# A two-layer graph network on one core: the edge attributes turned by VectorE in 32 x 32 squares, with a slot of a tile holding 128 consecutive edges

## The chip, the cores and the metric

One core of a Trainium2 chip. The metric is the device time of one execution in microseconds; the span is the part of it between the first and the last instruction that the profile shows. Engines are named TensorE (PE; PEld is its weight load), VectorE (DVE), ScalarE (ACT), GpSimd (POOL) and SyncE (SP).

## The reference

12,500 nodes with 64 features, 200,000 edges sorted by target, 32 attributes per edge. All in float32.

```python
# layer 0
x_t = leaky_relu(x @ W1n + b1n) @ W2n + b2n                 # nodes
e_t = leaky_relu(edge_attr @ W1e + b1e) @ W2e + b2e         # edges: 32 -> 64 -> 64
agg = segment_sum(x_t[src] * e_t * dp_scale, dst)
x   = layernorm(x + (layernorm(x + agg * res_w) * gamma + beta))
# layer 1: 8 relations, weights from 4 bases
xw  = x @ (w_comp @ weight)                                 # one table of rows per relation
agg = segment_sum(xw[edge_type, src] * edge_weight, dst)
out = layernorm(x + relu(agg + h_bias))
```

## The kernel before

A **tile** is 512 edges, J = 4 **slots** of 128, one edge to a partition. 390 whole tiles are worked off in 195 **pairs** (V = 2 tiles), and a tail of 320 edges is the 196th. Ten tiles are a **body**, five pairs a **half**; each loop iteration is two halves. In the kernel before, partition p of a tile holds the four consecutive edges 4p to 4p+3, one in each slot.

**Before the edges.** The node network fills `node_table` in HBM. Meanwhile the lists `dst`, `src`, `edge_type` and `edge_weight` are loaded, 512 to a row, cast by GpSimd, and turned by TensorE (`turn`, L1272 to L1279), so that an edge's number comes to lie on its partition; VectorE makes the target numbers relative to the tile's first (`relative`), ScalarE copies the sources and weights out of PSUM, VectorE makes the row numbers of layer 1 (`row_of`). The sources of the first ten tiles come by a DMA of their own straight into `src_ix`, so that gathers can begin as soon as `node_table` is written.

**Layer 0, one step per pair p.** The five engines run the same order of steps, written out by hand, and meet by semaphores only:

- GpSimd (`gather`, L571): four indirect DMAs per tile bring 128 rows of 256 bytes each into one of ten slots of `rows`. A tile may be fetched when the message of the tile ten before is made (`msg_ready`).
- SyncE (L425): loads the attributes of a half (640 KB) into one of two halves of `attr`, when those of the half before it in the same place are turned.
- TensorE (`step0`, L1376 and after): scatters pair p, tile by tile (L1347: messages times one-hot, summed over the edges, into PSUM); second matmuls of the edge network for pair p+2 (L1332 for the bias, L1339); first matmuls for pair p+3 (L1323, `attrT` against `W1e_d`, into `ps_z`); then turns the attributes of pair p+4 (L1315, two transposes of 128 x 128 into `ps_T`).
- ScalarE (`step`): `low` = 0.1 z + 0.1 b of the first matmuls (L639) for pair p+2, then the copy of the turned attributes of pair p+3 from `ps_T` to `attrT` (L630), by which columns are also put in order.
- VectorE (`step0`, L1147 and after): `hid` = max(z + b, low) for pair p+2 (L1029); message of the odd tile of pair p (L1054: gathered rows times `ps_o`); adds the even tile's sums to `acc` (L983); one-hot of pair p+1 (L972); message of the even tile of pair p+1; adds the odd tile's sums.

`attrT`, `ps_z` and `low` exist once, so the chain first matmuls, `low`, `hid`, second matmuls, first matmuls goes round once per pair. In places fixed by a table of limits (`final`), a chunk of 5 blocks of nodes that can get no further edges is finished between steps: turned, normed (VectorE, 14 steps), and its rows for layer 1 are made in three parts (TensorE `rel_products` against ScalarE `rel_copies`) and stored.

**Layer 1** has no edge network: gathers from `rel_table`, messages, scatter, add, and the last normalisation.

The lines of the step that the change touches:

```python
def edge_copy(p):                                            # ScalarE
    act.wait_ge(transposed, p + 1 if is_fixed(p) else count(p))
    nc.scalar.copy(attrT[...], ps_T[...]).then_inc(attr_copied, 1)

def attr_transpose(p, u, turns):                             # TensorE
    for t in range(width(p)):
        last = nc.tensor.transpose(ps_T[...], attr[..., t * P : (t + 1) * P], ident[:])
    last.then_inc(transposed, 1)
```

Of the kernel before, what the change touches and what calls it, by code (L numbers as in the profile page):

```python
# [5 lines left out]
def bass_gnn_resnorm_d2_kernel(  # L6
# [46 lines left out]
    P = 128  # L53
# [15 lines left out]
    assert TAIL_P * J == E - FULL * ST and 0 < TAIL_P < P  # L69
    BODY = 10  # L70
# [23 lines left out]
    src_begin = src[0 : BODY * ST].rearrange("(s p j) -> p s j", p=P, j=J)  # L94
    weight_flat = edge_weight.rearrange("e o -> (e o)")
    attr_groups = edge_attr[0 : FULL * ST, :].rearrange("(g s p r) k -> g p s (r k)", s=HALF, p=P, r=V * J)
# [3 lines left out]
    with ctx:  # L100
# [54 lines left out]
        x_pair = rows[:, 0, :, :].rearrange("p (k b) f -> p k (b f)", k=2)  # L155
        attrT = sb("attrT", [P, V * P])
# [122 lines left out]
        src_first = sem("src_first")  # L279
        gathered = [[sem(f"gathered{l}_{u}") for u in range(BODY)] for l in range(2)]  # L280
        transposed = sem("transposed")
        attr_copied = sem("attr_copied")
# [118 lines left out]
        def _(sp):  # L401
# [22 lines left out]
            def load_attr(h, g):  # L424
                sp.dma_start(attr[:, h, :, :], attr_groups[g]).then_inc(attr_loaded[h], 16)  # L425
# [31 lines left out]
            def layer0_loads():  # L457
                sp.reg_mov(done, 0)
                with sp.Fori(0, LOOPS - 1) as i:
                    for h in range(2):  # L460
                        sp.wait_ge(transposed, i * TURN + (h + 1) * HALF)
                        load_attr(h, i * 2 + (2 + h))
                        next_chunk(sp, done, limit, i * 2 + h, store_rel)
                sp.wait_ge(transposed, (BODIES - 2) * HALF)
                load_attr(0, BODIES - 1)
                next_chunk(sp, done, limit, BODIES - 3, store_rel)
                sp.wait_ge(transposed, (BODIES - 1) * HALF)
# [13 lines left out]
            sp.dma_start(src_ix[:, :, :], src_begin).then_inc(src_first, 16)  # L481
# [24 lines left out]
        def _(pool):  # L506
# [37 lines left out]
            for q in range(PAIRS):  # L544
# [6 lines left out]
                stage(q)  # L551
                if ZERO_FIRST <= q < ZERO_FIRST + ZERO_PARTS:
# [4 lines left out]
            def gather(l, t):  # L557
# [5 lines left out]
                if l == 0 and t == 0:  # L563
                    pool.wait_ge(src_first, 16)
                if l == 0 and t == BODY:
                    pool.wait_ge(list_taken, 5)
# [19 lines left out]
        def _(act):  # L586
# [28 lines left out]
            node_lower(PAIRS - 1, 0)  # L615
            act.wait_ge(s_edge_const, 16 * len(EDGE_CONSTS))
# [9 lines left out]
            def edge_copy(p):  # L626
                w = width(p) * P
                act.wait_ge(transposed, p + 1 if is_fixed(p) else count(p))
                if width(p) == V:
                    nc.scalar.copy(  # L630
                        attrT[:, :].rearrange("k (t q c) -> k c t q", t=V, c=V),
                        ps_T[:, 0:w].rearrange("k (c t q) -> k c t q", t=V, c=V),
# [902 lines left out]
```

## Time and profile before

| | |
|---|---|
| median of 3 runs | 5004.18 us (4999.41 to 5016.95) |
| profiled execution | 5002.53 us |
| its span | 5000.7 us |
| instructions | 33,996 |
| busy | PE 2157.5, PEld 1454.3, DVE 1585.2, ACT 380.7, POOL 2994.8 us |
| DMA | 175,940 packets, 169.74 MB |
| chain that ended last | another core or an unknown queue 23%, issue 22%, PE 11%, DVE 9% |

The busy time of an engine is the time in which one of its instructions ran; register, branch and semaphore instructions aren't counted. A matmul's end is modelled. "PEclk" is the clock that TensorE was granted, as a share of 2.4 GHz. In a row of the timeline stand the start, the time until the last of the merged instructions ended, engine, line, operation, tiles, shapes and count, and in brackets how long the engine was idle before and what released it; "remote" and "issue" are releasers that the profile can't name.

### The profile page before, as it was taken

What the parts mean: (1) busy time and instruction counts of PE and PEld (TensorE: products, weight loads), DVE (VectorE), ACT (ScalarE), POOL (GpSimd) and SP (SyncE); (2) the same over time, 40 slices, a digit from 0 to 9 for tenths busy, and PEclk for the clock granted to TensorE, in tenths of its full rate; (3) what the DMA queues carried; (4) which work ended last, traced back from release to release, by engine and by line L of the source; (5) the groups of instructions that cost most, each with busy time, mean ns of one, the idle gap of its engine ahead of it and who ended that gap; (6) DMA issues with size and microseconds to landing.
All of it is one profiled execution on the core that took longest, in us unless ns stands there. A gap on an engine that the chain in (4) does not pass through costs nothing.

```text
span 5000.7 us, 33996 instructions
## 1 busy us (share of the span) xinstructions
PE 2157.5 (43%) x7388; PEld 1454.3 (29%) x7389; DVE 1585.2 (32%) x3586; ACT 380.7 (8%) x879; POOL 2994.8 (60%) x3219
## 2 busy tenths in 40 slices
PE   6444454555555555565555233332333332232323
PEld 5333333333333433343332111121222221121222
DVE  4222232323333333343332122232322233233234
ACT  2100010101111111111111000000000000000000
POOL 5566665556555655555543676667666666666654
PEclk7777776777777777776775555555555555555556
DMA  4111111111111111121111111111111111111111
GB/s 101 29 32 32 32 33 42 31 43 42 42 41 38 45 42 46 32 52 41 51 37 39 23 25 22 24 23 25 23 25 25 25 24 25 24 24 26 25 25 21
DMA packets 175940, 169.74 MB, mean 34 GB/s; under 512 B 84098, under 2 KB 111606, under 8 KB 175630
## 3 DMA queue, kind: packets, MB, share of 16 engines
q0 software_dynamic: 100096, 102.60, 11.6%
q1 hardware_dynamic: 75246, 64.45, 4.2%
q14 instruction: 299, 2.45, 0.2%
q8 instruction: 11, 0.18, 0.0%
q10 hardware_dynamic: 288, 0.07, 0.0%
HBM read 134.80 MB, written 32.10 MB: 33 GB/s over the span
## 4 chain that ended last, share of the span: by engine, by line
another core or an unknown queue 23%; issue 22%; PE 11%; DVE 9%; DVEq 8%; ACT 1%; POOL 1%; ACTq 0%; DMA 0%; SPq 0%
PE ps_agg L1347 4%; DVE acc L983 3%; DVEq L965 2%; DVE work L1054 2%; DVE work L972 2%; PE ps_fin L1431 1%; PE ps_o L1339 1%; DVEq L983 1%; PE ps_z L1323 1%; DVEq L996 1%; DVEq L987 1%; PE ps_agg L1431 1%; POOL rows L571 1%; PE ps_T L1420 1%
## 5 line engine op out<-in xcount | busy, mean ns | idle before, releaser
L571 POOL DMA_INDIRECT rows<-node_table,acc x1524 | 1441.6, 946 | 1029.5 <-DVE work L1054 587.8
L571 POOL DMA_INDIRECT rows<-rel_table,row_ix x1564 | 1479.1, 946 | 886.1 <-issue 467.3
L1347 PE MATMUL ps_agg<-work 128*128 128x256 f32 x2348 | 906.9, 536 | 1658.1 <-DVE work L1054 1239.9
L1347 PEld LDWEIGHTS ps_agg<-work 128*128 128x128 f32 x2348 | 573.5, 265 | 1942.2 <-DVE work L1054 1324.1
L972 DVE TENSOR_TENSOR work<-ps_x,rel 128x1024 f32<-128x1024 f32 x392 | 479.0, 1222 | 535.9 <-issue 425.0
L983 DVE TENSOR_TENSOR acc<-acc,ps_agg 64x128 f32 x1174 | 333.7, 284 | 868.8 <-remote 627.9
L1029 DVE SCALAR_TENSOR_TENSOR hid<-ps_z,b1e_c,low 128x512 f32<-128x512 f32 x196 | 147.1, 751 | 1225.9 <-ACT low L639 994.2
L1347 PE MATMUL ps_z<-work 128*128 128x256 f32 x392 | 178.3, 602 | 489.6 <-DVE work L1054 313.7
L1054 DVE TENSOR_TENSOR work<-rows,ps_o 128x256 f32<-128x256 f32 x782 | 323.1, 413 | 81.4 <-DMA rows<-rel_table,row_ix 43.5
L1339 PE MATMUL ps_o<-W2e_d,hid 128*128 128x128 f32 x1564 | 299.4, 350 | 0.0
L1339 PEld LDWEIGHTS ps_o<-W2e_d,hid 128*128 128x128 f32 x1564 | 255.8, 248 | 64.1 <-issue 64.1
L1347 PEld LDWEIGHTS ps_z<-work 128*128 128x128 f32 x392 | 104.9, 293 | 555.5 <-DVE work L1054 344.4
L1347 PE MATMUL ps_T<-work 128*128 128x256 f32 x388 | 168.3, 580 | 193.3 <-issue 128.2
L1323 PE MATMUL ps_z<-attrT,W1e_d 128*128 128x256 f32 (+1 forms) x784 | 236.7, 431 | 0.5 <-ACT attrT L630 0.5
L639 ACT ACTIVATE low<-ps_z,b1e_low 128x512 f32<-128x512 f32 x196 | 134.6, 687 | 1277.6 <-remote 872.5
L1402 PE MATMUL ps_fin<-fold,acc 128*128 128x64 f32 x392 | 74.0, 358 | 282.0 <-ACT acc L675 183.1
L1347 PEld LDWEIGHTS ps_T<-work 128*128 128x128 f32 x388 | 108.2, 294 | 244.0 <-issue 147.3
L1323 PEld LDWEIGHTS ps_z<-attrT,W1e_d 128*128 128x128 f32 x784 | 160.3, 228 | 16.9 <-ACT attrT L630 0.9
L1402 PEld LDWEIGHTS ps_fin<-fold,acc 128*128 128x128 f32 x392 | 69.1, 268 | 303.0 <-issue 303.0
L983 DVE TENSOR_TENSOR acc<-acc,ps_T 64x128 f32 x194 | 55.2, 284 | 311.4 <-remote 216.4
L983 DVE TENSOR_TENSOR acc<-acc,ps_z 64x128 f32 x196 | 55.7, 284 | 239.4 <-remote 139.6
L655 ACT COPY ps_o<-enorm 128x40 f32 (+2 forms) x40 | 7.7, 196 | 1500.2 <-issue 809.5
(136 smaller groups left out, 1304.4 us busy)
## 6 DMA issues: line engine op xcount, KB each, us to landing
rows<-rel_table,row_ix POOLq DMA_INDIRECT x1564
attr<-in_edge_attr_dram SPq DMA_DIRECT2D x39, 640.0 KB
rows<-node_table,acc POOLq DMA_INDIRECT x1524
rel_table<-acc SPq DMA_DIRECT2D x19, 1280.0 KB
node_table<-work SPq DMA_DIRECT2D x24, 128.0 KB, 2.0
out_dram<-x_sb SPq DMA_DIRECT2D x19, 160.0 KB
x_sb<-in_x_dram SPq DMA_DIRECT2D x1, 768.0 KB, 6.9
acc<-in_dst_dram SPq DMA_DIRECT2D x1, 768.0 KB
```

Of the source, the lines that this page charges most:

```text
L571: nc.gpsimd.indirect_dma_start(rows[0:n, t % BODY, j, :], None, table, bass.IndirectOffsetOnAxis(ap=lists[0:n, t, j : j + 1], axis=0),).th ...
L639: nc.scalar.activation(low_pair, ps_z[:, :], ACT.Identity, bias=b1e_low[:], scale=SLOPE).then_inc(low_ready, 1)
L965: dve.reg_load([further[r]] + window[r][0 : width(p)], control[0:1, bass.ds(p, 1), 0 : 1 + width(p)].rearrange("p o v -> p (o v)"),)
L972: return nc.vector.tensor_tensor(o, iota_ps.rearrange("p (o n) -> p o n", o=1).to_broadcast([P, q, P]), r.rearrange("p (j o) -> p j o", o= ...
L983: last = nc.vector.tensor_tensor(a, a, bank[f, at + g * P : at + (g + 1) * P], ALU.add)
L1029: nc.vector.scalar_tensor_tensor(hid_pair, ps_z[:, :], b1e_c[:], low_pair, ALU.add, ALU.max).then_inc(hid_ready, 1)
L1054: nc.vector.tensor_tensor(msg[:, u % 2, v * J : (v + 1) * J, :], tile, factor, ALU.mult).then_inc(msg_ready[l][v], 1)
L1323: last = nc.tensor.matmul(ps_z[:, pr * V * P : pr * V * P + w], W1e_d[:, pr, :], attrT[:, 0:w], start=True, stop=True)
L1339: last = nc.tensor.matmul(bank[:, at : at + P], hid_pair[:, z : z + P], W2e_d[:], start=False, stop=(t == w - 1 and pr == 1), skip_group_c ...
L1347: last = nc.tensor.matmul(bank[:, 0 : 2 * P], data[:, 2 * jj : 2 * jj + 2, :], hot[:, 2 * jj : 2 * jj + 2, :], start=(jj == 0), stop=(jj = ...
L1402: nc.tensor.matmul(ps_fin[:, b * F : (b + 1) * F], block, fold[:], start=True, stop=True,).then_inc(block_turned[l], 1)
L1431: nc.tensor.matmul(ps_rel[b % 2][:, :], xT[:, b % 2, :], rel_w[:].rearrange("p r f -> p (r f)"), start=True, stop=True,).then_inc(rel_made, 1)
```

## The change

The transposes on TensorE and the copies on ScalarE go. VectorE turns a pair's attributes instead, one instruction of 128 x 256 from `attr` to `attrT`, in which each square of 32 partitions by 32 columns is turned in its place. `attr` is loaded with four edges (128 columns) per partition and tile, in runs of 512 bytes where they were 1,024. A square turned so leaves attribute k of 32 edges, four apart, in 32 columns; the first matmuls put their columns in the edges' order by reading `attrT` in the order (tile, q, j), with a step of 32 elements between neighbours. Of the 128 partitions of `attrT`, 32 each hold 128 consecutive edges, so a slot is now 128 consecutive edges, and all lists turn to match: `turn` reads its 128 columns in one run, no longer every fourth. The sources of the first ten tiles are loaded as the other lists are, cast by GpSimd in the node network's loop, turned by TensorE behind it and copied by ScalarE. The tail has three slots (128, 128 and 64 edges) where it had four of 80, so three gathers per layer, and its small copies and subtractions are two instead of one.

```diff
-    attr_groups = edge_attr[0 : FULL * ST, :].rearrange("(g s p r) k -> g p s (r k)", s=HALF, p=P, r=V * J)
+    attr_groups = edge_attr[0 : FULL * ST, :].rearrange("(g s p j) k -> g p s (j k)", s=V * HALF, p=P, j=J)
...
-            sp.dma_start(src_ix[:, :, :], src_begin).then_inc(src_first, 16)
+            sp.dma_start(first_i, src_begin).then_inc(first_loaded, 16)
...
+                if q == CAST_FIRST - 1:
+                    pool.wait_ge(first_loaded, 16)
+                    nc.gpsimd.tensor_copy(first_f, first_i).then_inc(first_cast, 1)
...
+            act.wait_ge(first_turned, 1)
+            nc.scalar.copy(
+                src_ix[:, :, :], ps_fin[:, 0 : J * BODY].rearrange("p (j t) -> p t j", j=J)
+            ).then_inc(first_taken, 1)
...
-                n = P if t < FULL else TAIL_P
-                for j in range(J):
+                for j, n in enumerate(TAIL_ROWS if t == FULL else [P] * J):
+                    if n == 0:
+                        continue
...
             def step(p):
                 if not is_fixed(p):
                     edge_lower(p)
-                    edge_copy(p)
...
-            link(relative(rel[0:TAIL_P, FULL : FULL + 1, :], turned[0:TAIL_P, n : n + 1, :], FULL, 1))
+            for j, p in ((slice(0, TAIL_FULL), P), (slice(TAIL_FULL, TAIL_FULL + 1), TAIL_REST)):
+                link(relative(rel[0:p, FULL : FULL + 1, j], turned[0:p, n : n + 1, j], FULL, 1))
...
+            def attr_turn(p, u, turns):
+
+                if u % HALF == 0:
+                    dve.wait_ge(attr_loaded[u // HALF % 2], (turns + 1) * 16)
+                    dve.sem_inc(turns_begun, 1)
+                nc.vector.transpose(attrT[:, :], attr[:, u // HALF % 2, u % HALF, :]).then_inc(attr_turned, 1)
...
                 message(0, p, u, 1)
+                if not is_fixed(p) or p + 3 <= LAST:
+                    attr_turn(p + 3, (u + 3) % TURN, i + (u + 3) // TURN)
                 add_sums(0, p, u, 0)
...
-                m, at = (TAIL_P, R_REST) if c == RCH - 1 else (P, 0)
-                by_column = raw_lists[0:rows_c, n, c, :].rearrange("p (e j) -> p e j", j=J)
-                for j in range(J):
+                sizes, at = (TAIL_ROWS, R_REST) if c == RCH - 1 else ([P] * J, 0)
+                for j, m in enumerate(sizes):
...
-            def attr_transpose(p, u, turns):
...
             def edge_first(p):
                 w = width(p) * P
-                pe.wait_ge(attr_copied, count(p, 0))
+                by_edge = attrT[:, 0:w].rearrange("k (t j q) -> k t q j", j=J, q=DE)
+                pe.wait_ge(attr_turned, count(p, 0))
                 for pr in range(2):
                     last = nc.tensor.matmul(
-                        ps_z[:, pr * V * P : pr * V * P + w], W1e_d[:, pr, :], attrT[:, 0:w], start=True, stop=True
+                        ps_z[:, pr * V * P : pr * V * P + w], W1e_d[:, pr, :], by_edge, start=True, stop=True
...
-                if not is_fixed(p) or p + 4 <= LAST:
-                    attr_transpose(p + 4, (u + 4) % TURN, i + (u + 4) // TURN)
```

VectorE in a step of layer 0's loop, from `hid` to the one-hot, before:

```order
L1029 SCALAR_TENSOR_TENSOR hid<-ps_z,b1e_c,low 128x512 [waits low_ready]
L1054 TENSOR_TENSOR work<-rows,ps_o 128x256 [waits gathered0_3,added0_1]
L987 ISA [waits scattered0_0]
L983 TENSOR_TENSOR acc<-acc,ps_agg 64x128
L983 ISA
L983 TENSOR_TENSOR acc<-acc,ps_agg 64x128
L965 ISA
L965 TENSOR_LOAD control
L972 ISA [waits added0_0]
L972 TENSOR_TENSOR work<-ps_x,rel 128x1024
L1054 TENSOR_TENSOR work<-rows,ps_o 128x256 [waits mm2_done,gathered0_4]
```

and with the change:

```order
L1034 SCALAR_TENSOR_TENSOR hid<-ps_z,b1e_c,low 128x512 [waits low_ready]
L1067 TENSOR_TENSOR work<-rows,ps_o 128x256 [waits gathered0_3,added0_1]
L1043 STREAM_TRANSPOSE attrT<-attr 128x256
L992 ISA [waits scattered0_0]
L988 TENSOR_TENSOR acc<-acc,ps_agg 64x128
L988 ISA
L988 TENSOR_TENSOR acc<-acc,ps_agg 64x128
L970 ISA
L970 TENSOR_LOAD control
L977 ISA [waits added0_0]
L977 TENSOR_TENSOR work<-ps_x,rel 128x1024
L1067 TENSOR_TENSOR work<-rows,ps_o 128x256 [waits mm2_done,gathered0_4]
```

Between the message of the odd tile and the addition of the even tile's sums stands the turn, with no wait of its own but once in a half, for the load.

TensorE in a step of the loop, from the second matmuls of pair p+2 to the scatter of the next pair, before:

```order
L1332 MATMUL ps_o<-b2e,ones 128x512 [waits hid_ready]
L1339 MATMUL ps_o<-W2e_d,hid 128x128 x4
L1323 MATMUL ps_z<-attrT,W1e_d 128x256 [waits attr_copied]
L1323 MATMUL ps_z<-attrT,W1e_d 128x256
L1315 MATMUL ps_T<-ident,attr 128x128 x2
L1385 ISA
L1354 TENSOR_LOAD control
L1347 MATMUL ps_agg<-work 128x256 [waits msg_ready0_0]
L1347 MATMUL ps_agg<-work 128x256
```

and with the change:

```order
L1351 MATMUL ps_o<-b2e,ones 128x512 [waits hid_ready]
L1358 MATMUL ps_o<-W2e_d,hid 128x128 x4
L1342 MATMUL ps_z<-attrT,W1e_d 128x256 [waits attr_turned]
L1342 MATMUL ps_z<-attrT,W1e_d 128x256
L1402 ISA
L1373 TENSOR_LOAD control
L1366 MATMUL ps_agg<-work 128x256 [waits msg_ready0_0]
L1366 MATMUL ps_agg<-work 128x256
```

The transposes are gone, and the first matmuls wait for VectorE's turn (`attr_turned`) in place of ScalarE's copy (`attr_copied`).

ScalarE in two steps of the loop, before:

```order
L639 ACTIVATE low<-ps_z,b1e_low 128x512 [waits mm1_done]
L630 COPY attrT<-ps_T 128x2x128 [waits transposed]
L647 REGISTER_ALU
L639 ACTIVATE low<-ps_z,b1e_low 128x512 [waits mm1_done]
L630 COPY attrT<-ps_T 128x2x128 [waits transposed]
L647 ISA
L333 TENSOR_LOAD final
```

and with the change:

```order
L647 ACTIVATE low<-ps_z,b1e_low 128x512 [waits mm1_done]
L654 REGISTER_ALU
L647 ACTIVATE low<-ps_z,b1e_low 128x512 [waits mm1_done]
L654 ISA
L342 TENSOR_LOAD final
```

Each `low` has lost the copy behind it; in the steps with a part of a chunk the exchange with TensorE follows there.

## Rows read from the trace of the kernel before

**Rows 1.** The page: busy us, share of the span and instructions of each engine.

```profile
PE 2157.5 (43%) x7388; PEld 1454.3 (29%) x7389; DVE 1585.2 (32%) x3586; ACT 380.7 (8%) x879; POOL 2994.8 (60%) x3219
```

**Rows 2.** Stretches: start:end, length, busy of each engine (count), PEclk, DMA share, GB/s.

```profile
1500.00:2000.00 500.00, 275.65 (x1027) 185.42 (x1028) 177.86 (x388) 69.64 (x153) 290.08 (x307) 0.73 0.18 43
```

**Rows 3.** Groups by line and form, 400 to 2,700 us: busy us, mean ns | idle before, releasers.

```profile
L972 DVE TENSOR_TENSOR work<-ps_x,rel 128x1024 f32<-128x1024 f32 x175 | 214.3, 1225 | 72.4 <-DVE acc L983 43.0 <-issue 20.4
L1323 PE MATMUL ps_z<-attrT,W1e_d 128*128 128x256 f32 x688 | 205.8, 428 | 0.0
L983 DVE TENSOR_TENSOR acc<-acc,ps_agg 64x128 f32 x700 | 199.1, 284 | 334.6 <-remote 209.1 <-PE ps_agg L1347 82.3 <-issue 31.8
L1054 DVE TENSOR_TENSOR work<-rows,ps_o 128x256 f32<-128x256 f32 x349 | 143.2, 410 | 0.0
...
L1029 DVE SCALAR_TENSOR_TENSOR hid<-ps_z,b1e_c,low 128x512 f32<-128x512 f32 x173 | 129.8, 751 | 1046.2 <-ACT low L639 834.2 <-issue 208.4 <-DVE acc L1106 3.3
```

**Rows 4.** Timeline, 1,500 to 1,531 us, two steps and the idle time behind them.

```profile
1503.64 0.69 ACT L639 ACTIVATE low<-ps_z,b1e_low 128x512 f32<-128x512 f32 x1 [14.81 <-remote]
...
1505.71 0.95 POOL L571 DMA_INDIRECT rows<-node_table,acc  x1 [5.20 <-DVE work L1054]
...
1507.30 0.41 DVE L1054 TENSOR_TENSOR work<-rows,ps_o 128x256 f32<-128x256 f32 x1
...
1510.89 0.69 ACT L639 ACTIVATE low<-ps_z,b1e_low 128x512 f32<-128x512 f32 x1 [6.29 <-PE ps_z L1323]
1510.90 1.03 PE L1347 MATMUL ps_agg<-work 128*128 128x256 f32 x4
...
1512.74 1.13 PE L1347 MATMUL ps_agg<-work 128*128 128x256 f32 x4 [0.81 <-issue]
...
1515.11 1.03 PE L1323 MATMUL ps_z<-attrT,W1e_d 128*128 128x256 f32 x4
...
1524.47 0.95 POOL L571 DMA_INDIRECT rows<-node_table,acc  x1 [0.31 <-issue]
1528.45 0.69 ACT L639 ACTIVATE low<-ps_z,b1e_low 128x512 f32<-128x512 f32 x1 [16.60 <-remote]
...
1530.52 0.95 POOL L571 DMA_INDIRECT rows<-node_table,acc  x1 [5.10 <-DVE work L1054]
```

**Rows 5.** Timeline, 72 to 134 us, the first gathers and the start of layer 0's loop.

```profile
72.47 1.14 POOL L571 DMA_INDIRECT rows<-node_table,src_ix  x1 [8.50 <-DMA node_table<-work]
...
101.50 0.18 ACT L731 CAST acc<-ps_fin 128x24 int32<-128x24 f32 x1 [14.87 <-remote]
...
111.33 0.69 DVE L940 SCALAR_TENSOR_TENSOR row_ix<-acc,ps_o 128x512 int32<-128x512 int32 x1 [25.17 <-issue]
...
132.12 0.66 PE L1315 MATMUL ps_T<-ident,attr 128*128 128x128 f32 x2 [1.16 <-ACT enorm L732]
132.82 0.38 ACT L630 COPY attrT<-ps_T 128x256 f32<-128x256 f32 x1 [1.58 <-PE ps_T L1315]
...
133.25 2.07 PE L1323 MATMUL ps_z<-attrT,W1e_d 128*128 128x256 f32 x4 [0.47 <-ACT attrT L630]
```

**Rows 6.** Who waited for whom, 400 to 2,700 us: us in total, times, longest.

```profile
DVE hid L1029 <- ACT low L639: 834.2, 106, 14.6
...
ACT low L639 <- remote: 706.3, 52, 19.4
POOL rows L571 <- DVE work L1054: 518.1, 102, 10.8
```

**Rows 7.** Line 1315, the transposes: duration ns min/median/max, first and last start us, forms.

```profile
L1315 PEld LDWEIGHTS ps_T<-ident,attr x391: 139/142/230, 132.1 to 2623.5; 128*128 128x128 f32 x196
L1315 PE MATMUL ps_T<-ident,attr x391: 272/273/445, 132.1 to 2623.7; 128*128 128x128 f32 x196
```

**Rows 8.** Line 1279, the list transposes, 74 to 84 us: durations, then the stretch with PEclk.

```profile
L1279 PEld LDWEIGHTS ps_o<-ident,acc x24: 195/226/231, 74.7 to 83.6; 128*128 128x128 f32 x24
...
74.00:84.00 10.00, 9.29 (x48) 7.94 (x48) 0.50 0.17 28
```

More of the change, by code:

```diff
@@ L69, in bass_gnn_resnorm_d2_kernel @@
     assert TAIL_P * J == E - FULL * ST and 0 < TAIL_P < P
+    TAIL_ROWS = [min(P, max(0, E - FULL * ST - j * P)) for j in range(J)]
+    TAIL_FULL = TAIL_ROWS.count(P)
+    TAIL_REST = TAIL_ROWS[TAIL_FULL]
+    assert TAIL_REST and not any(TAIL_ROWS[TAIL_FULL + 1 :]) and P == J * DE
     BODY = 10
@@ L155, in bass_gnn_resnorm_d2_kernel @@
         x_pair = rows[:, 0, :, :].rearrange("p (k b) f -> p k (b f)", k=2)
+        first_i = rows[0:BODY, 4:6, :, :].rearrange("p t j f -> p (t j f)").bitcast(i32)
+        first_f = rows[0:BODY, 6:8, :, :].rearrange("p t j f -> p (t j f)")
         attrT = sb("attrT", [P, V * P])
@@ L624, in count @@
                 return lead
[L626 to L632, printed above, removed]
-                    ).then_inc(attr_copied, 1)
-                else:
-                    nc.scalar.copy(attrT[:, 0:w], ps_T[:, 0:w]).then_inc(attr_copied, 1)
             def edge_lower(p):
@@ L731, in _ @@
                     nc.scalar.copy(o[:, c * P : c * P + t, :], turned[:, 0:t, :]).then_inc(list_taken, 1)
-                nc.scalar.copy(o[0:TAIL_P, FULL, :], turned[0:TAIL_P, t, :]).then_inc(list_taken, 1)
+                for j, p in ((slice(0, TAIL_FULL), P), (slice(TAIL_FULL, TAIL_FULL + 1), TAIL_REST)):
+                    nc.scalar.copy(o[0:p, FULL, j], turned[0:p, t, j]).then_inc(list_taken, 1)
             act.reg_mov(tabled, 0)
@@ L950, in _ @@
                     dve.sem_inc(row_taken, 1)
-            link(row_of(row_ix[0:TAIL_P, FULL, :], src_turned[0:TAIL_P, FULL, :], turned[0:TAIL_P, n, :]))
+            for j, p in ((slice(0, TAIL_FULL), P), (slice(TAIL_FULL, TAIL_FULL + 1), TAIL_REST)):
+                link(row_of(row_ix[0:p, FULL, j], src_turned[0:p, FULL, j], turned[0:p, n, j]))
             dve.sem_inc(row_taken, 1)
@@ L1035, in message @@
                 if is_fixed(p):
-                    dve.wait_ge(gathered[l][slot], (p // HALF + 1) * TILE_GATHERS)
+                    of_tile = TILE_GATHERS if p < LAST else 16 * (TAIL_FULL + 1)
+                    dve.wait_ge(gathered[l][slot], p // HALF * TILE_GATHERS + of_tile)
                 else:
@@ L1180, in step1, with half @@
                     dve.reg_add(lead, lead, 1)
-            def half(l, k, h, first, finish_chunk):
+            def half(l, k, h, i, first, finish_chunk):
                 for u in range(HALF):
-                    (step0, step1)[l](first + u, h * HALF + u)
+                    (step0, step1)[l](first + u, h * HALF + u, i)
                     if u == NORM_AFTER:
@@ L1260, in _ @@
             node_second(PAIRS - 1, 0)
+            pe.wait_ge(first_cast, 1)
+            for j in range(J):
+                last = nc.tensor.transpose(
+                    ps_fin[:, j * BODY : (j + 1) * BODY], first_f[:, j * P : (j + 1) * P], ident[0:BODY, 0:BODY])
+            last.then_inc(first_turned, 1)
             pe.wait_ge(s_spans, 1)
@@ L1292, in _ @@
             pe.wait_ge(node_out, PAIRS)
+            pe.wait_ge(first_taken, 1)
             for n in (DST, SRC, TYPE, WEIGHT):
```

66 lines of the change are left out of this document (32 added, 34 removed).

## The prediction

> **What bounds the kernel now.** I read the page's totals first, then the stretches, the groups and waits of layer 0, and last single steps of the timeline. No engine is full: GpSimd is busy for 60% of the span, TensorE for 43%, VectorE for 32%, ScalarE for 8% [rows 1]. The change's loop work lies in layer 0 alone, of which a stretch of 500 us shows GpSimd busy for 290, TensorE for 276, and a mean granted clock of 0.73 [rows 2]. In it a pair of tiles costs 2,300 / 173 = 13.3 us (173 is the count of `hid` between 400 and 2,700 us [rows 3]).
>
> Two things make up those 13.3 us. The first is GpSimd. From the gather at 1505.71 to the one at 1524.47 there are 15 steps of 1.25 us, of which 0.95 busy [rows 4], so the 8 gathers of a pair are 10.0 us, 195 pairs 1,950 us in each layer. That is a floor which the change leaves alone, but for one gather fewer in each layer's tail. The second is a wait which no busy row explains. At 1515.11 TensorE issues the first edge matmul, and the row says it is done 1.03 us later; yet ScalarE's `low`, which waits for it, starts at 1528.45, releaser "remote" [rows 4]. Meanwhile GpSimd gathers without a pause from 1505.71 to 1525.4, goes idle because all ten slots are full, and takes up again at 1530.52, when VectorE's message has freed a slot [rows 4]. So a turn is 24.8 us (1505.71 to 1530.52) for 16 gathers, two pairs: 20 us of gathers and 5 us until messages flow again. In the first 40 gathers, which begin at 72.47 us, the same is seen without edge matmuls: steps that wait for a TensorE transpose come at 101.50 on ScalarE and at 111.33 on VectorE, after idle times of 14.87 and 25.17 us [rows 5]. What holds TensorE's completions back the trace doesn't say; it shows that they come late when gathers have run for some 8 us on end, and at once before. The waits agree: between 400 and 2,700 us `hid` waited 834 us for `low`, `low` 706 us for "remote", the gathers 518 us for messages [rows 6].
>
> **The loop that the change cuts into.** In a step that isn't held back, the chain is: first matmuls, `low` (0.69 [rows 4]), `hid` (0.75), message of the odd tile (0.41 [rows 3]), its scatter, second matmuls, first matmuls. From `low` at 1503.64 to `low` at 1510.89 it takes 7.25 us [rows 4].
>
> **The change part by part.**
> TensorE loses 391 transposes of 273 ns and their weight loads, issued in pairs [rows 7]. In the step at 1510 they stand behind the first matmuls, followed by the scatter of the even tile (1510.90, 1.03 us); then TensorE sits idle for 0.81 us until the message of the odd tile lets it go on at 1512.74 [rows 4]. The two transposes (0.38 us of matmuls) are thus beside `low`, `hid` and message; at the full clock they give 0. At the lower clock one transpose is up to 445 ns [rows 7] and the first matmuls of a pair take 2.07 instead of 1.03 us [rows 5, 4]. One of them takes 428 ns in the mean; at the upper level four overlapping ones take 1.03 us, about 380 each, and at the lower they take twice that. So 13 to 25% run at the lower level: one pair in five. Where it lasts into the scatter, the transposes are some 0.45 us late and have 0.81 less what the slower scatter takes of it, so that I put 0.2 us a pair on the path: 39 pairs x 0.2 = **-8 us**, between 0 and -17.
>
> ScalarE loses 195 copies of 0.38 us [rows 5], which stand behind `low` in its order and before nothing that is late in a plain step: 0. In the steps with a part of a chunk (3 for each of 19 chunks, 57) the copy and the transposes stand ahead of a serial exchange between TensorE and ScalarE over 98 blocks, which is on the path; there 0.35 us goes each time: -20 us, of which a held-back completion swallows half: **-10 us**.
>
> VectorE gains 196 turns of 128 x 256 float32. The trace has no such instruction. Its nearest rows bound it: 284 ns for 128 columns, 410 ns for 256 (two inputs), 1,225 ns for 1,024 [rows 3]; I take 410, since its output is as large, and keep 284 and 1,225 (196 of them: 56 to 240 us of VectorE's time). It goes between the message of the odd tile and the addition of the even one. Behind it are that addition, the one-hot, and the next pair's even message. That message was done at 1507.71, and TensorE came for it at 1510.90 [rows 4]: 3.2 us of cover, more than any end. TensorE comes for the turned attributes only behind a scatter and the second matmuls (1512.74 to 1515.11 [rows 4]), 2 us after the turn has ended. GpSimd waits for the odd message, ahead of the turn. So 0; were that cover gone, it would be +80 us (196 x 0.41). The DMA wait for the attributes moves with the turn from TensorE to VectorE, where messages are queued behind it, but the load is asked for six steps before: at 13.3 us a step nothing waits. The Trainium skill's "VectorE: DVE Perf Modes" (The three transpose paths) gives 311 ns for 128 x 128 in bf16; no run here shows it, and by it two such would be 0.62 us, also covered.
>
> The first matmuls now read `attrT` with a step of 32 elements between neighbours, 784 of them [rows 3], and these **are** on the chain. No moving operand of the trace is read so. The nearest rows are the list transposes, whose stationary operand has a step of 4 elements: 226 ns at the median for a load, 231 at most, in a stretch at a granted 0.50 [rows 8], against 142 at the median and at most 230 for the contiguous ones, whose longest are those at the lower clock [rows 7]. So a broken row costs nothing at 1.2 GHz; at 2.4 GHz nothing is shown. I take 0. The other end is that a step read holds the pace of 1.2 GHz at 2.4 GHz: 2.07 - 1.03 = +1.04 us a pair.
>
> Around the loop: attribute loads stay 640 KB each, in runs of 512 B instead of 1 KB, with five pairs of time to land: 0. The first lists are cast, turned and copied (three steps of fewer elements than the smallest bound of the turn), beside the wait of the first gather for the node table, which ends at 72.47: 0 to +1. The list turning has one more small copy or subtraction three times on its serial way: +0.5 us. At the loop's start transposes and copy fall off the way (132.12 to 133.25 [rows 5]): -1.1 us. A gather less in each tail: -1.25 us for the last, the one of layer 0 is covered by layer 1's table.
>
> **Sum.** -8 -10 +0 +0 +0.5 -1.1 -1.25 = -20 us; of a turn 20 of 24.8 us are GpSimd's and are not shortened, so part of this is hidden again, I take 40% (+8): **-12 us**. The profiled execution took 5002.53 us, its span 5000.7 and 1.8 around it; the median of three runs is 5004.18. That gives 4990.5 against the profiled one and **4992** against the median. A measurement of this kernel can tell about 0.3% (15 us) from no change, so that is no change.
>
> **The rivals.**
> *Step reads are slow at the full clock.* Four fifths of the pairs (156) pay 1.04 us on the chain: 162 us, if no gather covers it; half if the 20 us of gathers do. Range +60 to +160, middle about 5090. For it: the first matmuls are on the chain, and no row shows a step in a moving operand. Against: the loads of [rows 8] cost nothing extra. It decides as soon as the four matmuls take over 1.2 us at 2.4 GHz. The Trainium skill's "SBUF — State Buffer" (SBUF cachelines) states this rule: full speed only while at least two accesses hit the same 16-byte line. By it every column would pay; the loads of [rows 8], a line for each element, do not show it at the lower clock. Chance 0.25.
> *A step out of the held-back turns.* If a chain some tenths shorter finishes one more step before completions are held back, more pairs go into a turn: three pairs for 30 + 5 us is 11.7 instead of 12.4 us a pair. With one turn in two so, 97 pairs x 0.7 = -68 us: 4936. For it: `low` at 1510.89 made it, the next at about 1516 didn't. Against: at the full clock I find nothing shorter on the chain. Together with gains of mine that aren't hidden (-15 to -40): chance 0.34.
> *VectorE becomes the chain.* If the turn takes 1.2 us and finds VectorE behind, as after a chunk's normalisation (19 times ten us), or if TensorE, with less to do, is granted the lower clock more often than now (0.73 [rows 2]), +15 to +50 us. Chance 0.05.
> *No change*, the forecast: 0.36.
>
> **How the numbers follow.** Within 0.3%: 0.36. Faster: 0.34. Slower: 0.25 + 0.05 = 0.30. The range reaches down to the second rival's turns (4925) and up to the middle of the first one's (5090); outside it lie the dearest step reads (0.1) and a gain that nothing here prices (0.08).
>
> **What would show it.** Right: the transposes and copies are gone, the turn takes near 0.41 us with next to no wait behind it; four first matmuls still take about 1.03 us at 2.4 GHz; gathers still come in runs of about 16 with some 5 us between; `hid` still waits for `low`. Wrong: first matmuls near 2 us at the full clock (first rival); longer runs of gathers and GpSimd busier than 0.58 of layer 0 (second); one-hots or TensorE waiting for VectorE's turn (third).

## The result: 0.6% to 1% faster, in the steps that finish a chunk

The changed kernel takes 4959.2 us at the median of six runs, the kernel before 4997.07 beside it: a ratio of 0.9941 (95% interval 0.9917 to 0.9964). A second comparison, told below, gave 0.9905 (0.9869 to 0.9941). The forecast was 4992 us and "no change"; the range of 4925 to 5090 holds the result, the likeliest case missed it. The profiled execution has a span of 4957.5 us, against 5000.7 before.

The page of the kernel after, answering to [rows 1], and the 500 us of [rows 2]:

```profile
PE 2247.0 (45%) x6997; PEld 1417.5 (29%) x6998; DVE 1642.9 (33%) x3784; ACT 326.0 (7%) x686; POOL 2995.4 (60%) x3218
```

```profile
1500.00:2000.00 500.00, 299.43 (x964) 179.86 (x965) 192.23 (x431) 59.05 (x114) 296.93 (x314) 0.74 0.18 45
```

TensorE has 391 matmuls fewer and is busy for 90 us more. The reason is in the groups by line and form, 400 to 2,700 us, which answer to [rows 3]:

```profile
L586 POOL DMA_INDIRECT rows<-node_table,acc x1359 | 1287.2, 947 | 863.7 <-DVE work L1067 467.7 <-issue 396.0
L1342 PE MATMUL ps_z<-attrT,W1e_d 128*128 128x256 f32 x688 | 330.7, 614 | 0.0
...
L1043 DVE STREAM_TRANSPOSE attrT<-attr 128x256 f32<-128x256 f32 x173 | 75.8, 438 | 3.5 <-issue 3.5
```

The first matmuls (L1342) take 614 ns in the mean where they took 428 (the transposes, which are gone, took back part of that). VectorE's turn (L1043) takes 438 ns, and all idle time ahead of its 173 rows is 3.5 us. The durations of line 1342 over the whole run, and below them line 1323 of the kernel before:

```profile
L1342 PE MATMUL ps_z<-attrT,W1e_d x784: 383/617/764, 135.1 to 2589.6; 128*128 128x256 f32 x195, 128*128 128x128 f32 x1
```

```profile
L1323 PE MATMUL ps_z<-attrT,W1e_d x784: 275/379/793, 133.3 to 2637.6; 128*128 128x256 f32 x195, 128*128 128x128 f32 x1
```

The last first matmul starts at 2589.6 us in place of 2637.6: 48 us, more than the whole gain of the span, come from layer 0. Behind it the changed kernel takes 2367.9 us and the one before 2363.1.

What the step read costs depends on the clock. Four first matmuls of the changed kernel, and the stretch around them with its granted clock of 1.00 (answering to 1.03 us at 1515.11 in [rows 4], also at 1.00):

```profile
1521.20 1.92 PE L1342 MATMUL ps_z<-attrT,W1e_d 128*128 128x256 f32 x4
```

```profile
1521.10:1523.20 2.10, 2.02 (x7) 0.71 (x5) 0.00 (x0) 0.00 (x0) 1.61 (x2) 1.00 0.18 31
```

Over the 135 pairs that lie wholly at that clock (137 before) one matmul takes 615 ns at the median, against 379. Over the 12 that lie wholly at a granted 0.50 (20 before) it takes 617 ns, against 634.

**Where in layer 0.** I took the distances between every fifth start of `hid`, from the third one on, which gives 38 halves of five pairs, and kept apart the 17 in which a chunk's normalisation starts and the other 21. A half without a chunk takes 60.9 us in the mean before and 61.3 after; one with a chunk 69.3 and 65.8. So the gain is some 3.5 us in each of 17 halves, and nothing in a plain step. (The expectations below were written with a count of the halves that differs at the ends, and so say 61.5 and 66.3.)

**What differs there.** In these halves TensorE and ScalarE exchange blocks: two transposes of a block, ScalarE's copy of it, products, copies (52 exchanges in layer 0's loop, behind three steps of each chunk). One of them in the timeline of the kernel before; ScalarE's copy waits for the two transposes at 1571.90:

```profile
1571.59 0.38 PE L1315 MATMUL ps_T<-ident,attr 128*128 128x128 f32 x2
1571.90 0.43 PE L1420 MATMUL ps_T<-ident,acc 128*64 128x128 f32 x2
...
1573.12 0.95 POOL L571 DMA_INDIRECT rows<-node_table,acc  x1 [2.31 <-DVE work L1054]
...
1576.87 0.95 POOL L571 DMA_INDIRECT rows<-node_table,acc  x1 [0.30 <-issue]
1579.53 0.26 ACT L711 COPY work<-ps_T 64x128 f32<-64x128 f32 x1 [14.36 <-remote]
1579.85 0.69 PE L1420 MATMUL ps_T<-ident,acc 128*64 128x128 f32 x2 [7.51 <-ACT work L711]
```

and the same exchange, the sixteenth, after:

```profile
1549.86 0.43 PE L1437 MATMUL ps_T<-ident,acc 128*64 128x128 f32 x2
...
1551.18 0.26 ACT L716 COPY work<-ps_T 64x128 f32<-64x128 f32 x1 [8.31 <-PE ps_T L1437]
1551.49 0.43 PE L1437 MATMUL ps_T<-ident,acc 128*64 128x128 f32 x2 [1.20 <-ACT work L716]
```

7.63 us from TensorE's transposes to ScalarE's copy, or 1.32. It is of the kind that the prediction described for `low`: TensorE is done by its row, and the engine that waits for it goes on only when gathers have stopped. But it isn't held back by a single run of over 8 us, as the prediction has it. The transposes start in a stop of GpSimd, which lasts 2.31 us, behind 16 gathers; the copy comes 1.7 us after the four gathers behind that stop. The waits, 400 to 2,700 us, count them; of before (its other rows are [rows 6]):

```profile
ACT work L711 <- remote: 254.6, 20, 15.1
```

and of after:

```profile
DVE hid L1034 <- ACT low L647: 898.7, 117, 14.5
...
ACT low L647 <- remote: 696.7, 57, 16.2
POOL rows L586 <- DVE work L1067: 467.7, 99, 10.7
...
ACT work L716 <- remote: 176.3, 13, 14.6
```

Those for `low` are no fewer. Those for an exchange's copy ("work <- remote") fall from 20 to 13. Below, an exchange is **late** when its first copy starts over 2 us behind the start of its first transpose: 20 of 52 before, 14 after; the distances add up to 157.5 and 112.1 us. These 45 us are nearly all that layer 0 gained: from its first `hid` to its last it takes 2513.9 us before and 2463.9 after.

### The profile page after: what moved, and what is told of

The parts are those of the page before. It is cut to its first block, busy times and chain, and to the rows that moved or that the text cites. A ratio compares the mean times of both kernels' runs of the same rounds, so it can differ in the third digit from the quotient of the medians.

```text
span 4957.5 us, 33259 instructions
## 1 busy us (share of the span) xinstructions
PE 2247.0 (45%) x6997; PEld 1417.5 (29%) x6998; DVE 1642.9 (33%) x3784; ACT 326.0 (7%) x686; POOL 2995.4 (60%) x3218
## 4 chain that ended last, share of the span: by engine, by line
another core or an unknown queue 22%; issue 17%; DVE 10%; DVEq 8%; PE 8%; POOL 1%; ACT 1%; ACTq 0%; DMA 0%; SPq 0%
DVE acc L988 3%; DVEq L970 3%; PE ps_agg L1366 2%; DVE work L1067 2%; DVE work L977 2%; PE ps_fin L1448 1%; PE ps_z L1342 1%; POOL rows L586 1%; DVEq L988 1%; PE ps_o L1358 1%; DVEq L1001 1%; DVEq L992 1%; PE ps_agg L1448 1%; DVEq L977 1%
## 5 line engine op out<-in xcount | busy, mean ns | idle before, releaser
L1366 PEld LDWEIGHTS ps_agg<-work 128*128 128x128 f32 x2348 | 591.7, 268 | 1951.2 <-DVE work L1067 1309.0
L1342 PE MATMUL ps_z<-attrT,W1e_d 128*128 128x256 f32 (+1 forms) x784 | 376.2, 613 | 1.2 <-DVE attrT L1043 1.2
L1342 PEld LDWEIGHTS ps_z<-attrT,W1e_d 128*128 128x128 f32 x784 | 162.5, 230 | 80.6 <-issue 69.1
L1448 PE MATMUL ps_fin<-rel_w,work 64*128 64x512 f32 x118 | 84.0, 799 | 73.2 <-ACT work L716 68.8
```

The source lines that it names most:

```text
L1342: last = nc.tensor.matmul(ps_z[:, pr * V * P : pr * V * P + w], W1e_d[:, pr, :], by_edge, start=True, stop=True)
L1366: last = nc.tensor.matmul(bank[:, 0 : 2 * P], data[:, 2 * jj : 2 * jj + 2, :], hot[:, 2 * jj : 2 * jj + 2, :], start=(jj == 0), stop=(jj = ...
L1448: nc.tensor.matmul(ps_rel[b % 2][:, :], xT[:, b % 2, :], rel_w[:].rearrange("p r f -> p (r f)"), start=True, stop=True,).then_inc(rel_made, 1)
```

## The experiments

Ratios are to runs of the kernel before on the same chip, and only ratios can be compared between chips: x_tc, x_t, x_c and x_contig ran on a chip on which the kernel before takes 4965 us, x_lay, x_turn, x_after and x_c2 on one where it takes 5000. The change itself was not run on the first of these. "Late" and "sum" are those of the exchanges, "plain" and "chunk" the us of a half, each from one profiled execution. In x_lay, x_turn and x_contig edges' columns and gathered rows stand in different orders, so that layer 0 sums other products.

| kernel | ratio (95% interval) | late | sum us | plain | chunk |
|---|---|---|---|---|---|
| before | 1 | 20 | 157.5 | 60.9 | 69.3 |
| layout alone, x_lay | 0.998 (0.996 to 1.0) | 21 | 142.1 | 60.8 | 68.8 |
| the change | 0.9941 (0.9917 to 0.9964) | 14 | 112.1 | 61.3 | 65.8 |
| the change again, x_after | 0.9905 (0.9869 to 0.9941) | 14 | 123.0 | 61.4 | 65.8 |
| turn alone, x_turn | 0.9906 (0.9872 to 0.9941) | 14 | 112.2 | 61.1 | 66.0 |
| hand-off put back, x_tc | 0.9958 (0.9934 to 0.9982) | 14 | 117.8 | 60.3 | 67.3 |
| transposes put back, x_t | 0.995 (0.9922 to 0.9978) | 15 | 105.7 | 60.6 | 66.1 |
| spare copy, x_c | 0.9881 (0.9843 to 0.992) | 8 | 72.5 | 60.8 | 63.6 |
| spare copy again, x_c2 | 0.9894 (0.9851 to 0.9936) | 14 | 113.0 | 60.7 | 66.7 |
| reads in one run, x_contig | 0.9938 (0.9914 to 0.9961) | 17 | 137.3 | 60.7 | 66.0 |
| pause per pair, x_pause | 0.957 (0.9538 to 0.9602) | 3 | 37.4 | 56.0 | 63.7 |
| pause per tile, x_pause_tile | 1.0353 (1.0325 to 1.0381) | 0 | 25.8 | 69.3 | 70.9 |
| pause in both layers, x_pause_both | 0.9681 (0.9656 to 0.9707) | 3 | 38.6 | 56.5 | 63.6 |
| before, with pause, x_before_pause | 0.9558 (0.952 to 0.9597) | 15 | 69.3 | 57.3 | 63.5 |

The sums track the time of layer 0: the time from its first `hid` to its last, less the sum of the exchanges, is 2345 to 2362 us in nine of the ten traces without a pause. The tenth is x_contig's, with 2317.

**What the removed work was worth.** Theory A was that transposes and copy, ahead of the exchange, were what cost.

```diff
 # TensorE, behind edge_first(p + 3); x_t and x_tc
+                for t in range(width(p)):                 # p is here the step's p + 4
+                    last = nc.tensor.transpose(ps_T[:, t * P : (t + 1) * P], ident[:], ident[:])
+                last.then_inc(transposed, 1)
 # ScalarE, behind edge_lower(p); x_tc
+                act.wait_ge(transposed, p + 1 if is_fixed(p) else count(p))
+                nc.scalar.copy(spare_space[:, 0:w], ps_T[:, 0:w]).then_inc(spare_copied, 1)
 # TensorE, edge_first; x_tc
                 pe.wait_ge(attr_turned, count(p, 0))
+                pe.wait_ge(spare_copied, count(p, 0))
```

> The changed kernel with the hand-off of before put back beside VectorE's turn: TensorE turns two squares of the identity into ps_T where it turned the attributes, ScalarE copies 128 x 256 from there behind every low and waits for it, and the first matmuls wait for that copy too. Added work, same output. Theory A (mine): the gain of 38 us came from the steps with a part of a chunk, where transposes and copy stood ahead of the exchange between TensorE and ScalarE. Then 30 to 60 us come back, nearly all in the halves with chunks (66.3 us a half goes to about 69), plain halves stay at 61.5: 4990 to 5020 us. Rival B: the gain came from the layout (slots of 128 consecutive edges, lists, loads, tail). Then nothing comes back, or only a few us: 4955 to 4970 us. Rival C: the step reads cost much everywhere and were paid by a larger gain in every plain step. Then with both costs the kernel is slower than before, over 5040 us, and the plain halves lengthen by over 1 us.

> The changed kernel with two spare transposes of the identity per pair on TensorE, into ps_T, at the place of those taken out; nobody waits for them. Added work, same output. Theory A (TensorE's queue ahead of the exchange): each of the chunk steps is 0.4 to 0.9 us longer, 57 to 95 of them, so +10 to +40 us against the change: 4970 to 5000 us. Rival D (only the hand-off matters: a copy that waits for a TensorE completion that is held back): nothing, 4955 to 4965 us.

x_tc came out at 0.9958 and x_t at 0.995, both between the change and the kernel before, and both intervals overlap with those of the change: 8 to 26 us came back in x_tc, where A wanted 30 to 60, and 4 to 22 in x_t. The chunk halves of x_tc are at 67.3 us (A: about 69), late exchanges stay at 14 and 15. B's "nothing, or a few us" isn't excluded by x_tc alone; C is, since x_tc is not slower than before. x_t, where A wanted 10 to 40 us and D nothing, decides between neither. So the work itself, its place in the order and its waits don't give the whole gain; whether they give none or half of it, these two runs can't tell.

```diff
 # ScalarE, behind edge_lower(p); x_c and x_c2
+                act.wait_ge(spare_copied, p + 1 if is_fixed(p) else count(p))
+                nc.scalar.copy(
+                    spare_space[:, 0:w], W1e_d[:, :, :].rearrange("p a b -> p (a b)")[:, 0:w]
+                ).then_inc(spare_copied, 1)
```

> The changed kernel with a copy of 128 x 256 on ScalarE behind every low, from one constant to unused space, waiting for nobody and awaited by nobody. Added work, same output. Theory A: ScalarE reaches the chunk's exchange 0.35 us later in the chunk steps: +5 to +20 us, 4965 to 4980 us. Rival D (the copy's wait for TensorE was what cost): nothing, 4955 to 4962 us.

> The changed kernel with a spare copy on ScalarE behind every low, once more: the first time it was 0.9881 of before (0.9843 to 0.992), faster than the change, with 0.38 us more work in every step. Theory K (chance among few runs): 0.992 to 0.997, as the change beside it. Theory L (the copy does something good, such as delaying ScalarE's next reading of a semaphore until TensorE's completion is there): 0.985 to 0.991, below the interval of the change beside it.

No cost that could be measured: the copy's 0.38 us are hidden, against theory A. At first it even looked better than the change; repeated beside the change it is at 0.9894 against 0.9905, well inside that interval, as K's condition wants and L's excludes. K's figure was missed and L's was hit, since the change beside it was itself faster than the 0.992 expected. The two profiles of this one kernel picture the spread: spans of 4918.8 and 4953.9 us, of which the two chips make a part, with 8 and 14 late exchanges and sums of 72.5 and 113.0.

**The step of 32 in the first matmuls.**

```diff
-                by_edge = attrT[:, 0:w].rearrange("k (t j q) -> k t q j", j=J, q=DE)
+                by_edge = attrT[:, 0:w]
```

> The changed kernel with attrT read in one run of 256 by the first matmuls instead of with a step of 32. The edges' columns then stand in another order than the gathered rows, so layer 0 sums other products; the same number of instructions and bytes. Theory A: a first matmul takes 380 ns at 2.4 GHz in place of 617, a step that is not held back is 0.8 us shorter (7.3 in place of 8.1), which plain halves hide behind gathers and chunk halves do not: -15 to -60 us against the change, 4900 to 4945 us. Rival E (gathers hide it everywhere): 4950 to 4965 us. Rival F (it is on the chain in every pair): 195 x 0.8 = -156 us, 4800 to 4830 us.

Line 1342 is then as before the change (275/379/767 ns):

```profile
L1342 PE MATMUL ps_z<-attrT,W1e_d x784: 275/379/767, 131.8 to 2575.5; 128*128 128x256 f32 x195, 128*128 128x128 f32 x1
```

and the ratio is 0.9938, between the change's two. Theory E holds for the time: 0.9 us less in each step at the full clock bought nothing that could be measured in it. F is out by 150 us, and A's lower half too. The trace leaves room for two effects that cancel: with 17 late exchanges and a sum of 137.3 us, 14 to 25 more than in the change, layer 0 still takes no longer (2454.3 us from first to last `hid`, against 2463.9 and 2467.8). It is the one kernel outside the band given under the table, by some 30 us. One profile can't settle whether the shorter matmuls gave these.

**The change in two parts.** One has the layout (loads, lists, tail, first lists) without the turn, the other the turn without the layout. x_lay is the changed kernel with this (lines cut to their core):

```diff
-                    attr_turn(p + 3, (u + 3) % TURN, i + (u + 3) // TURN)           # VectorE
...
+                    edge_copy(p)                               # ScalarE
...
+                    attr_transpose(p + 4, (u + 4) % TURN, i + (u + 4) // TURN)      # TensorE
...
-                by_edge = attrT[:, 0:w].rearrange("k (t j q) -> k t q j", j=J, q=DE)
+                by_edge = attrT[:, 0:w]
```

x_turn is the kernel before with this:

```diff
-                    edge_copy(p)                               # ScalarE
...
-                    attr_transpose(p + 4, (u + 4) % TURN, i + (u + 4) // TURN)      # TensorE
...
+                    attr_turn(p + 3, (u + 3) % TURN, i + (u + 3) // TURN)           # VectorE
...
-                        ps_z[...], W1e_d[:, pr, :], attrT[:, 0:w], start=True, stop=True
+                        ps_z[...], W1e_d[:, pr, :], by_edge, start=True, stop=True
```

> The change without its turn: layout, loads in runs of 512 bytes, lists, first lists, three slots in the tail as changed, but TensorE transposes the attributes, ScalarE copies them and the first matmuls read attrT in one run, as before. Columns and gathered rows then stand in different orders, so layer 0 sums other products; instructions and bytes are the same. Theory B (the layout gives the gain, as the kernel with the hand-off put back suggests: 0.9958 of before): a ratio of 0.992 to 0.996. Theory G (moving the turn from TensorE and ScalarE to VectorE gives it): 0.998 to 1.002. Theory H (neither: a shift of some tenths of a us at any place reshuffles the turns of 16 gathers): both halves of the change between 0.992 and 1.0, and their gains don't add up to that of the whole.

> The kernel before with VectorE's turn in place of TensorE's transposes and ScalarE's copies, and first matmuls that read attrT with a step of 32, but layout, loads (runs of 1,024 bytes), lists and four slots of 80 in the tail as before. Layer 0 sums other products. Theory B: 0.998 to 1.002 of before. Theory G: 0.992 to 0.996. Theory H: between, and not additive.

> The changed kernel itself once more, beside the others on their chip. All theories: 0.992 to 0.997 of before. If it comes out at 0.998 or above, the gain that is to be explained was smaller than the first interval said.

Turn alone 0.9906, the whole change 0.9905, layout alone 0.998 with 1.0 in its interval. Theory G: the gain is that of the moved turn, here somewhat larger than G (0.992 to 0.996) or anything expected of the change (0.992 to 0.997). The waits of x_lay and then of x_turn show what goes with it, 20 waits for copies that are held back, as before, or 14 (the change has 13):

```profile
ACT work L730 <- remote: 242.2, 20, 14.2
```

```profile
ACT work L697 <- remote: 187.8, 14, 14.6
```

**Does an unbroken run of gathers hold completions back?** All gains so far hang on that mechanism, which the prediction had only read from the trace. The next kernel adds two lines to the changed one:

```diff
 # GpSimd, gather(l, t)
+                if l in (0,) and t and t % 2 == 0:
+                    pool.wait_ge(gathered[l][(t - 1) % BODY], (t - 1) // BODY * TILE_GATHERS + TILE_GATHERS)
                 for j, n in enumerate(TAIL_ROWS if t == FULL else [P] * J):
```

x_pause_tile has `t % 1` for `t % 2`, so that it waits before every tile, and x_pause_both `l in (0, 1)`.

> The changed kernel in which GpSimd, in layer 0, waits before each pair of tiles until the rows of the tile before it have landed. That is a short pause (some 1 to 2 us, estimated from the wait at a full window) behind every 8 gathers, nothing else. Theory M: a run of gathers without a pause is what holds TensorE's completions back, from some 8 us into the run; a short pause lets them through. Then no step is held back for long, low follows the first matmuls within 1 us, a pair costs 10.0 + 1 to 2 us where it costs 12.3 in plain halves and 13.3 in those with a chunk: 80 to 250 us faster than the change, 4700 to 4870 us. Rival N: completions come only when gathers have stopped for some 3 us, whatever the pause: the pauses come on top, 195 x 0.5 to 1.5 us = 100 to 300 us slower, 5050 to 5250 us.

> As the kernel before it, with the pause in front of every tile, behind every 4 gathers. Theory M: a pair costs 10.0 + 2 x (1 to 2) us = 12 to 14 us, from no change to 300 us slower than the change, but low, hid and the exchanges of the chunks wait for no held-back completion. Rival N: 200 to 600 us slower, and low still late in every second step.

> As the first of these, with the pause per pair in both layers. Layer 1 has runs of over 30 gathers in its trace, its gathers wait for nothing in them, and it costs some 12 us a pair. Theory M: layer 1, whose scatter matmuls free the windows, gains too or stays: within -150 to +50 us of the kernel with the pause in layer 0 alone. Rival N: layer 1 is 100 to 300 us longer by its pauses.

x_pause takes 4785.49 us: 0.957 of before, by a wait that was added. Theory M holds and N falls, in the middle of M's forecast. The timeline of x_pause:

```profile
1499.72 1.94 PE L1344 MATMUL ps_z<-attrT,W1e_d 128*128 128x256 f32 x4
...
1501.70 0.69 ACT L649 ACTIVATE low<-ps_z,b1e_low 128x512 f32<-128x512 f32 x1 [9.74 <-issue]
...
1504.27 0.94 POOL L588 DMA_INDIRECT rows<-node_table,acc  x1 [0.31 <-issue]
...
1506.82 0.42 DVE L1069 TENSOR_TENSOR work<-rows,ps_o 128x256 f32<-128x256 f32 x1 [3.41 <-DMA rows<-node_table,acc]
...
1507.48 0.95 POOL L588 DMA_INDIRECT rows<-node_table,acc  x1 [2.27 <-DMA rows<-node_table,acc]
...
1511.70 1.94 PE L1344 MATMUL ps_z<-attrT,W1e_d 128*128 128x256 f32 x4
...
1513.67 0.69 ACT L649 ACTIVATE low<-ps_z,b1e_low 128x512 f32<-128x512 f32 x1 [11.29 <-issue]
```

`low` starts as the first matmuls end, in two steps running, at the cost of a pause of 2.27 us; [rows 4] had 12 us between them in every second step. Its waits, 400 to 2,700 us:

```profile
DVE work L1069 <- DMA rows<-node_table,acc: 579.3, 165, 5.2
...
DVE hid L1036 <- ACT low L649: 229.9, 38, 12.0
...
ACT work L718 <- remote: 23.9, 3, 8.1
```

`hid` waited 898.7 us for `low` and now waits 229.9, "low <- remote" (696.7) is gone, and messages wait for their rows instead, 579.3 us. Of the 176 us by which the span is shorter than the change's, 142 lie between the first and the last `hid` and 28 ahead of the first, where list turning runs beside the first 40 gathers (that part spreads: x_pause_both, the same program up to there, has its first `hid` at 101.3 us, x_pause at 110.1). A pause per tile costs more than it frees, as M allowed: 5177.11 us, 1.0353 (1.0325 to 1.0381), with no exchange late. That time fits M and N alike (both reached 200 to 300 us over the change); what speaks for M is that no exchange is late and that the longest wait of `hid` for `low` is 7.5 us. In layer 1 the pause only costs: x_pause_both takes 4838.95 us, 0.9681 (0.9656 to 0.9707), 53 us more than x_pause, just past what M had said (up to 50).

**What is left of the change without held-back completions?** The same pause in the kernel before:

> The kernel before with the same pause of GpSimd in front of every pair of layer 0: no turn on VectorE, transposes and copies in their old places. Theory Q (the change gains because the exchanges of the chunks meet fewer held-back completions): where the pause lets completions through, nothing is left to gain, and this comes out as the changed kernel with the pause did, 0.957 of before: 0.953 to 0.961, exchanges late in under 5 of some 49. Rival R (the change gains by the work it takes off TensorE and ScalarE, whatever is held back): its 0.6 to 0.9% stand on top, so this comes out at 0.963 to 0.968.

4783.26 us and 0.9558, against 0.957 for the changed kernel with the pause. Theory Q: nothing that can be measured is left of the gain; the two intervals allow 0.4% at most, and R's 0.963 lies above. One number missed: 15 exchanges are late, not under 5, though by less (sum 69.3 us). And in the traces layer 0 is not quite the same: from first to last `hid` x_before_pause takes 2343.0 us and x_pause 2321.6, with plain halves 1.3 us longer. An earlier first `hid` (98.5 against 110.1 us), which spreads by as much, and 7 us less behind the last make up for it. The last `hid` of x_before_pause comes 10 us later than that of x_pause, where without the pause it was 48 us, so that a small rest of the gain may be left in layer 0.

**How far into a run?** "Some 8 us" can be checked over all pairs, by the traces of the kernel before and of the changed one. I count a stop of GpSimd under 1.8 us as part of the run, and take only those first matmuls at whose end ScalarE has nothing else to do. Up to 8 us into a run, `low` follows within 1.5 us in 64 cases of 64 before and 66 of 66 after; further in, in none of 55 and none of 52. Exchanges that start further in are late in 15 cases of 15 before and 14 of 16 after; of those up to 8 us in, 3 of 34 are late before and none of 33 after. Without the 1.8 us, 10 and 7 of the late ones would stand up to 8 us into their run: 15 of these 17 follow a stop of 1.1 to 1.7 us, and 64 of the 65 that are on time there one of 2 us or more. So in these two traces a short stop doesn't let completions through, and one of over 2 us mostly does; the pause of x_pause is 2.27 us. The line isn't sharp: in x_c four exchanges behind a stop of 1.5 or 1.6 us are on time.

## Why the range held and the likeliest case did not

- **The bound** was read rightly: runs of 16 gathers, completions that come when these end. The same stall at the chunks' exchanges is where the change's gain lies. Breaking those runs up gave 3.5% on top of the change.
- **Transposes, -8 us**: put back alone, they cost 0.1 to 0.45% (4 to 22 us) against the two measurements of the change, with intervals that overlap. The term isn't refuted, its size isn't resolved.
- **ScalarE's copies, and 0.35 us at each of 57 exchanges, half of it swallowed, -10 us**: this is the step that failed. A copy put back costs nothing that could be measured, and yet the gain is in the halves with exchanges, 3.5 us in each of 17, over three times what I priced before halving. I took a held-back completion for something that swallows half of a saving. It is what makes the time there: a first copy came 0.5 us behind the transposes' start at the median or, held back, after 2 to 9 (7.63 us in the row above), and with the change 14 of 52 are of the second kind in place of 20. The price was to be set by how many exchanges meet one, not by the 0.35 us.
- **VectorE's turn, 410 ns, covered**: 438 ns, and 3.5 us of idle time ahead of it between 400 and 2,700 us. Right, and the third rival with it.
- **First matmuls, 0**: right for the time and wrong for the row. I gave +1.04 us a pair as the other end. At the full clock four of them take 1.92 us (the row above), where [rows 4] has 1.03; at a granted 0.50 they cost nothing more than before. The condition of the first rival came true (over 1.2 us), its +60 to +160 us did not. (The middle of that range would be 5114 us, and not the 5090 at which mine ended.) Its sentence "it decides as soon as" was wrong: in plain halves gathers cover it (60.9 to 61.3 us), and x_contig shows no cost in the whole time. That the range held is in part luck: the row on which its upper end rested came true, and cost nothing. The rule of the Trainium skill's "SBUF — State Buffer" (SBUF cachelines) is what the row shows at 2.4 GHz; that [rows 8] spoke against it was a reading at 1.2 GHz only.
- **Lists, start, tail, -1.85 us**: the first `hid` starts at 137.9 in place of 136.1 us, and what follows the last one takes 2356 in place of 2351. Too small to be told.
- **40% hidden again (+8)**: nothing in the traces answers to it. The gain stands in the number of late exchanges, and is not a share of what a step saves.
- **The second rival** (4936 us, 0.34) had the direction and the idea that fewer steps meet a stall. Its own mechanism, longer turns with three pairs in them, isn't there: between the first and the last `hid` there are 66 runs of 16 gathers before and 70 after, 4 and 2 of 20, and none of 24. Plain halves, where it would show, gain nothing. "GpSimd busier than 0.58 of layer 0", its other mark, came true (296.93 of 500 us against 290.08), but any shortening of layer 0 brings that about.

**Open.** Why the moved turn lets fewer exchanges be late isn't settled: transposes, copies and their waits, put back, don't bring back the 20, nor does the read in one run. Nor does the count above say it, by which 15 exchanges start over 8 us into a run before and 16 after. What the traces show is a shift: first matmuls end mostly 4 to 6 or 10 to 12 us into a run of gathers in the kernel before and in x_lay, 6 to 8 or 12 to 14 us in the change and in x_turn. It can't be all, since x_contig is back at 4 to 6 and 10 to 12 us, with 17 late exchanges and a ratio of 0.9938. Nor is it settled what in the chip holds TensorE's completions back, nor whether the stop of the issue or the landing of the rows lets them through: the pause does both, and no run parts them.

## What to carry to other kernels

When an engine waits for "remote" long after the row that it waits for has ended, look at what another engine is doing without a pause, and break that up once before shaving anything off the chain: here 2.3 us of pause per pair gave the kernel before 4.4% by itself, and each piece of 0.3 to 0.9 us per pair, put back or taken out by itself, moved the time by 0 to 0.5%. In such a kernel a saving is worth what it does to the number of steps that meet the stall; two profiles of one kernel (8 and 14 late exchanges) say how far one trace can be trusted for that.

## What the runs showed of the hardware

- Completions of TensorE's matmuls reached ScalarE late while GpSimd issued indirect DMAs without a pause (every 1.25 us). Where ScalarE was free, `low` followed the first matmuls within 1.5 us in 130 of 130 cases up to 8 us into a run of gathers and in none of 107 further in (kernel before and change together, stops under 1.8 us counted as part of a run). Waiting once per 8 gathers for the rows to land (2.3 us) let them through: 3 late exchanges of 52 in place of 14.
- A float32 moving operand of 128 x 256 read with a step of 32 elements: 615 ns at the median and 1.92 us for four at a granted 2.4 GHz, against 379 ns and 1.03 us in one run. At 1.2 GHz the medians are 617 ns with the step and 634 without: no cost.
- VectorE's turn of 128 x 256 float32 in squares of 32: 433 to 446 ns.
